# Re-ordering the front of a two-layer attention and expert kernel: clears, gate, row units and part loads

## The reference

```python
xn = _layernorm(x, axis=-1)
# attention, 16 heads of 16, causal
qkv = einsum('bsh,oh->bso', xn, w_qkv)            # q, k, v
scores = einsum('bhqd,bhkd->bhqk', q, k) * scale  # causal mask, softmax, times v, times w_o
# experts: 16 of them, 2 for each token
gate_scores = sigmoid(xn @ Wg.T + balance_bias)
topk_scores, topk_idx = lax.top_k(gate_scores, 2)
topk_scores = topk_scores / (topk_scores.sum(-1, keepdims=True) + 1e-06)
h = silu(einsum('td,edh->teh', xn, W1))
out = einsum('teh,te,ehd->td', h, combine, W2)
x = x + attention + experts
```

## Time and profile before

| | us |
|---|---|
| median of three runs | 1037.07 (1036.24 to 1037.13) |
| the profiled execution, its own time | 1040.66 |
| its span, first to last instruction | 1038.9 |
| PE busy | 903.0 (87% of the span) |
| DVE busy | 659.5 (63%) |
| ACT busy | 424.8 (41%) |
| POOL busy | 360.2 (35%) |
| mean granted TensorE clock | 0.93 of full |

### The profile page before, as it was taken

The page is one execution under the profiler, slowest core; times in us unless marked ns, Lnnn a source line. Parts: engine busy times, 40 slices in busy tenths (PEclk is TensorE's granted clock), DMA queues, the critical chain, the costliest instruction groups (busy, mean ns, idle before and its releaser), DMA issues. The chain is left out here.

```text
span 1038.9 us, 18184 instructions
## 1 busy us (share of the span) xinstructions
PE 903.0 (87%) x5962; PEld 482.8 (46%) x5963; DVE 659.5 (63%) x1561; ACT 424.8 (41%) x736; POOL 360.2 (35%) x541
## 2 busy tenths in 40 slices
PE   5577889999999999999999988889982799997763
PEld 3342223344444444444443322667440687786552
DVE  4257899887777787887877942758132444444444
ACT  3251245565655556555556666221120233331000
POOL 2121127413443325424242373002776000002775
PEclk9797589999999999999999989979997899999787
DMA  4855746230137312191110121900222354453443
GB/s 129 287 140 154 197 67 198 74 118 32 58 78 168 128 32 62 41 199 54 34 41 22 51 73 59 342 2 23 104 101 96 116 159 153 151 153 101 131 128 115
DMA packets 84136, 113.50 MB, mean 109 GB/s; under 512 B 12694, under 2 KB 72086, under 8 KB 83542
## 3 DMA queue, kind: packets, MB, share of 16 engines
q1 hardware_dynamic: 60966, 63.77, 21.8%
q0 software_dynamic: 13728, 37.50, 11.4%
q10 hardware_dynamic: 9360, 11.17, 3.3%
HBM read 58.11 MB, written 54.00 MB: 108 GB/s over the span
## 5 line engine op out<-in xcount | busy, mean ns | idle before, releaser
L732 ACT ACTIVATE probs<-ps_st 128x1024 f32<-128x1024 f32 (+3 forms) x320 | 286.2, 896 | 229.9 <-PE ps_st L1006 227.9
L856 DVE TENSOR_REDUCE part_max<-ps_row 128x1 f32<-128x512 f32 (+3 forms) x560 | 349.8, 668 | 46.7 <-PE ps_row L1022 23.4
L918 PE MATMUL ps_o<-probs,v_all 128*17 128x256 f32 (+1 forms) x2432 | 178.9, 367 | 2.8 <-POOL probs L629 2.5
L1226 POOL DMA_INDIRECT moe_yg<-yd,slot x64 | 61.5, 961 | 168.6 <-DMA yd<-moe_ys 149.4
L1022 PE MATMUL ps_row<-ks,qs 96*128 96x512 bf16 (+3 forms) x320 | 99.9, 377 | 16.7 <-DVE part_max L856 15.6
L1376 POOL DMA_INDIRECT xd<-xn,slot x64 | 64.0, 1000 | 91.6 <-DVE slot L209 72.5
L629 POOL TENSOR_SCALAR_AFFINE_SELECT probs<-probs 128x256 f32<-128x256 f32 x128 | 52.3, 411 | 125.2 <-ACT probs L732 124.0
L1022 PE MATMUL ps_row<-xt_ks,qs 96*128 96x512 bf16 (+3 forms) x320 | 92.5, 348 | 2.3 <-DVE part_max L856 0.9
L1006 PE MATMUL ps_st<-qs,ks 99*128 99x512 bf16 (+3 forms) x320 | 89.3, 362 | 4.4 <-DMA qs<-max_parts 4.4
L1006 PE MATMUL ps_st<-qs,xt_ks 99*128 99x512 bf16 (+3 forms) x320 | 88.1, 358 | 0.0
L918 PEld LDWEIGHTS ps_o<-probs,v_all 128*17 128x17 f32 x2432 | 40.7, 95 | 97.5 <-issue 88.4
(11 more groups left out here) (220 smaller groups left out, 1308.6 us busy)
## 6 DMA issues: line engine op xcount, KB each, us to landing
moe_xs<-xd SPq DMA_DIRECT2D x79, 128.0 KB, 2.1
yd<-moe_ys SPq DMA_DIRECT2D x79, 128.0 KB, 2.0
xd<-zeros SPq DMA_DIRECT2D x4, 2048.0 KB, 8.5
qk_parts<-probs SPq DMA_DIRECT2D x16, 384.0 KB, 4.1
qs<-qk_parts SPq DMA_DIRECT2D x96, 64.0 KB, 2.5
moe_xs<-xd POOLq DMA_DIRECT2D x47, 128.0 KB, 2.4
yd<-moe_ys POOLq DMA_DIRECT2D x47, 128.0 KB, 2.1
xd<-zeros ACTq DMA_DIRECT2D x2, 2048.0 KB, 13.0
```

The source lines that it names most:

```text
L732: act.activation(probs[:, at % NPB, :, off:CH], ps_st[at % 2][:, :, off:CH], ACT.Exp, scale=HD ** -0.5).then_inc(exp_done, 1)
L856: dve.tensor_reduce(part_max[reduced % 2][:, h:h + k, i, j:j + 1], bank[:, 0:k * w].rearrange("p (h w) -> p h w", h=k), AX_X, ALU.max).the ...
L918: mm = pe.matmul(ps_o[32 * q:32 * q + HD + 1, lo:hi], m.v_all[:, k, g * HG + q, :], probs[:, (at + q // 2) % NPB, q % 2, lo:hi], start=Fal ...
L1226: pool.indirect_dma_start(out=yg[:, i % YG, k, :], out_offset=None, in_=yd, in_offset=bass.IndirectOffsetOnAxis(m.r["slot"][:, k, i:i + 1], 0)
```

## The change

- **Clears.** The zeroing of `xd0` moves from ACT, after block 3, to SP, right behind the loads of x. The expert weights w1 and w2 are loaded by ACT at the start, behind the other weights, no longer after block 15.
- **Gate by chunk.** Bias, exponential, reciprocal, MAX8 and FIND_INDEX8 run for 4 tiles at a time. ACT makes the exponentials of chunks 0 and 1 ahead of the turned tokens of chunk 3, that of chunk 2 ahead of chunk 3's values, that of chunk 3 behind block 8.
- **Row units alternate with blocks.** Block 8 stands before row 0, 9 before row 3, 10 before row 6, 11 before row 9, 12 before row 11, 13 before row 13, 14 and 15 before row 16.
- **`rows_out(0, 0)`** is issued by ACT, between blocks 13 and 14, no longer by SP.
- **Parts by chunk.** `qk_parts` is laid out by part, chunk, output, token, and the outputs of a group are ordered position before head (the weights are reordered on the host), so a partition's load is one run of 4 KB. Terms that are neighbours are loaded together: three DMAs (of 3, 2 and 1 terms) for the keys of a chunk of the first group and three for the queries of a chunk of any group. Keys of later groups still take six DMAs.

```diff
+K_RUNS = [(0, 3), (3, 2), (5, 1)]
+Q_RUNS = [(0, 3, 0), (3, 2, 1), (5, 1, 2)]
+LOADS = len(K_RUNS)
...
-def load_keys(eng, m, g, tokens, done):
+def load_keys(eng, m, g, done):
+    rows = slice(D + g * HG * HD, D + (g + 1) * HG * HD)
     for t in range(TERMS):
-        src = m.qk_parts[K_PART[t], D + g * HG * HD:D + (g + 1) * HG * HD, tokens]
-        eng.dma_start(m.ks[g % 2][t * HD:(t + 1) * HD, :, tokens], src.rearrange("(h d) t -> d h t", d=HD)).then_inc(done, 16)
+        eng.dma_start(m.ks[g % 2][t * HD:(t + 1) * HD, :, :, :].rearrange("d c h t -> d c (h t)"),
+                      m.qk_parts[K_PART[t], :, rows, :].rearrange("c (d h) t -> d c (h t)", h=HG)).then_inc(done, 16)
+def load_chunk_of_keys(eng, m, g, c, done):
+    rows = slice(D + g * HG * HD, D + (g + 1) * HG * HD)
+    for first, count in K_RUNS:
+        eng.dma_start(m.ks[g % 2][first * HD:(first + count) * HD, c, :, :].rearrange("d h t -> d (h t)"),
+                      m.qk_parts[0:count, c, rows, :].rearrange("r (d h) t -> r d (h t)", h=HG)).then_inc(done, 16)
 def load_queries(eng, m, g, c, done):
-    for t in range(TERMS):
-        src = m.qk_parts[Q_PART[t], g * HG * HD:(g + 1) * HG * HD, c * CH:(c + 1) * CH]
-        eng.dma_start(m.qs[c][t * HD:(t + 1) * HD, :, :], src.rearrange("(h d) t -> d h t", d=HD)).then_inc(done, 16)
+    rows = slice(g * HG * HD, (g + 1) * HG * HD)
+    for first, count, part in Q_RUNS:
+        src = m.qk_parts[part, c, rows, :].rearrange("(d h) t -> d (h t)", h=HG)
+        eng.dma_start(m.qs[c][first * HD:(first + count) * HD, :, :].rearrange("d h t -> d (h t)"),
+                      src.unsqueeze(0).to_broadcast([count, HD, HG * CH])).then_inc(done, 16)
 def load_first_group(eng, m, c):
     for n in range(4 * c, 4 * c + 4):
         eng.wait_ge(m.parts_out[n], 16)
-    load_keys(eng, m, 0, slice(c * CH, (c + 1) * CH), m.first_in[c])
+    load_chunk_of_keys(eng, m, 0, c, m.first_in[c])
     load_queries(eng, m, 0, c, m.first_in[c])
 CLEAR = 16
-HEAD = 11
 TURNED = 16
+BLOCKS_BEFORE_ROW = {0: [8], 3: [9], 6: [10], 9: [11], 11: [12], 13: [13], 16: [14, 15]}
...
-    m.qk_parts = m.scratch("qk_parts", [PARTS, 2 * D, S], BF16)
+    m.qk_parts = m.scratch("qk_parts", [PARTS, C, 2 * D, CH], BF16)
...
+            sp.wait_ge(zero_ready, 1)
+            clear(sp, m, m.xd0, 0, NT0, m.cleared[0])
...
-                if n == 4 * C - 3:
-                    rows_out(0, 0)
...
+            act.dma_start(m.w1[:, :, :, :], a["w1"].rearrange("(k p) (e h) -> p k e h", p=P, e=E)).then_inc(m.moe0_w_in, 16)
+            act.dma_start(m.w2[:, :, :], a["w2"].rearrange("e p d -> p e d")).then_inc(m.moe0_w_in, 16)
...
-            act.wait_ge(zero_ready, 1)
-            clear(act, m, m.xd0, 0, NT0, m.cleared[0])
             turned_tokens(1)
             root(3)
             values_and_gate(1)
@@ -710,14 +731,18 @@
                 high_and_mid(n)
             turned_tokens(2)
             values_and_gate(2)
+            exp_of_gate(0)
+            exp_of_gate(1)
             turned_tokens(3)
+            exp_of_gate(2)
             values_and_gate(3)
-            act.wait_ge(logit_ready, 1)
-            act.activation(scores[:, :, :], scores[:, :, :], ACT.Exp, scale=-1.0).then_inc(exp_ready, 1)
-            for n in range(8, 16):
+            high_and_mid(8)
+            exp_of_gate(3)
+            for n in range(9, 14):
                 high_and_mid(n)
-            act.dma_start(m.w1[:, :, :, :], a["w1"].rearrange("(k p) (e h) -> p k e h", p=P, e=E)).then_inc(m.moe0_w_in, 16)
-            act.dma_start(m.w2[:, :, :], a["w2"].rearrange("e p d -> p e d")).then_inc(m.moe0_w_in, 16)
+            rows_out(act, 0, 0)
+            high_and_mid(14)
+            high_and_mid(15)
...
+            def gate_best(c):
+                cs = slice(c * TC, (c + 1) * TC)
+                dve.wait_ge(exp_ready, c + 1)
+                step.then(dve.tensor_scalar(scores[:, cs, :], scores[:, cs, :], 1.0, None, ALU.add))
+                step.then(dve.reciprocal(scores[:, cs, :], scores[:, cs, :]))
+                route_best(dve, step, r, scores, range(c * TC, (c + 1) * TC))
+            def before_row(n):
+                for block in BLOCKS_BEFORE_ROW.get(n, []):
+                    rest_of(block)
+                    if block == 8:
+                        gate_logits(C - 1)
+                    if block == 9:
+                        gate_best(C - 1)
+                    if block in (10, 11, 12):
+                        next(routing)
+                    if block == 13:
+                        route_to("masks")
+                    if block == 15:
+                        route_to("weights")
...
-                    pe.wait_ge(m.first_in[c], 16 * 2 * TERMS)
+                    pe.wait_ge(m.first_in[c], 16 * 2 * LOADS)
                     return
-                pe.wait_ge(q_in[c], 16 * TERMS * g)
+                pe.wait_ge(q_in[c], 16 * LOADS * g)
...
+                for block in BLOCKS_BEFORE_ROW.get(n, []):
+                    project_block(block)
```

More of the change, by code:

```diff
@@ L123, in norm_apply, with route_best @@
     step.sync()
+def route_best(dve, step, r, scores, tiles):
+    for i in tiles:
+        step(dve.max(r["best"][:, i, :], scores[:, i, :]))
+    step.sync()
+    for i in tiles:
+        step(dve.max_index(r["arg"][:, i, :], r["best"][:, i, :], scores[:, i, :]))
+    step.sync()
 def route(dve, step, r, scores, top, tiles, eps, factor, masks_ready, ranks_ready, ranks, slots_ready, ranks_read=None):
     best, arg, argf = r["best"], r["arg"], r["argf"]
[L132 to L139, removed]
     step.then(dve.tensor_copy(argf[:, :, :], arg[:, :, :]))
@@ L505, in used, with rows_out @@
             return sum(u[0] != "h" for u in rows[:n + 1])
+        def rows_out(eng, n, c):
+            eng.wait_ge(parts_ready, n + 1)
+            for part in range(PARTS):
+                eng.dma_start(qs[c][KROWS + part:KROWS + part + 1, :, :].rearrange("r h t -> r (h t)"),
+                              max_parts[n % 2][:, part, :]).then_inc(rows_in[n % 2], 16)
         @block.sync
         def _(sp):
[L510 to L514, removed]
             for c in range(C):
@@ L687, in values_and_gate, with exp_of_gate @@
                     act.copy(scores[:, i, :], ps_v[i % 2][:, D:D + E]).then_inc(v_copied, 1)
+            def exp_of_gate(c):
+                cs = slice(c * TC, (c + 1) * TC)
+                act.wait_ge(logit_ready, c + 1)
+                act.activation(scores[:, cs, :], scores[:, cs, :], ACT.Exp, scale=-1.0).then_inc(exp_ready, 1)
             def high_and_mid(n):
@@ L788, in before_plan @@
                 dve.wait_ge(b_in, 16)
-                dve.wait_ge(v_copied, T)
-                dve.tensor_tensor(scores[:, :, :], scores[:, :, :], bias.unsqueeze(1).to_broadcast([P, T, E]),
-                                  ALU.add).then_inc(logit_ready, 1)
[L792 to L808, removed]
-                if n == TURNED:
-                    rest_of(14)
-                    rest_of(15)
-                    route_to("weights")
+                for c in range(C - 1):
+                    gate_logits(c)
@@ new lines, in before_plan, with gate_logits @@
+                for c in range(C - 1):
+                    gate_best(c)
+            def gate_logits(c):
+                cs = slice(c * TC, (c + 1) * TC)
+                dve.wait_ge(v_copied, (c + 1) * TC)
+                dve.tensor_tensor(scores[:, cs, :], scores[:, cs, :], bias.unsqueeze(1).to_broadcast([P, TC, E]),
+                                  ALU.add).then_inc(logit_ready, 1)
+            def gate_best(c):
+                cs = slice(c * TC, (c + 1) * TC)
+                dve.wait_ge(exp_ready, c + 1)
+                step.then(dve.tensor_scalar(scores[:, cs, :], scores[:, cs, :], 1.0, None, ALU.add))
+                step.then(dve.reciprocal(scores[:, cs, :], scores[:, cs, :]))
+                route_best(dve, step, r, scores, range(c * TC, (c + 1) * TC))
@@ L829, in _ @@
                 n += 1
-                between_blocks(n)
+                before_row(n)
                 if u[0] == "h":
@@ L978, in _ @@
                 project_values(c)
-            for n in range(8, 12):
-                project_block(n)
             for u in plan:
-                if state["row"] == HEAD and state["exp"] == 0:
-                    project_block(12)
-                    project_block(13)
-                if state["row"] == TURNED and state["exp"] == 0:
-                    project_block(14)
-                    project_block(15)
                 if u[0] == "exp":
@@ L1477, in _ @@
                                         peak[:, :].unsqueeze(2).to_broadcast([P, T, E]), ALU.mult))
+            route_best(dve, step, r, scores, range(T))
             for _ in route(dve, step, r, scores, TOP1, NT1, 0.0, TOP1 / (TOP1 + 1), masks_ready, ranks_ready, 1,
@@ L1689, in experts_last, with width_before_head @@
         return w.transpose(1, 0, 2).reshape(w.shape[1], -1)
+    def width_before_head(w_t):
```

(4 more changed lines are left out.)

20 lines of the change are left out of this document (10 added, 10 removed).

## The result

| | before | after |
|---|---|---|
| median, us | 1036.65 (1035.38 to 1037.13) | 1053.66 (1049.5 to 1055.73) |
| ratio, 95% interval | | 1.0161 [1.0128, 1.0194] |
| profiled execution, its own time | 1040.66 | 1049.5 |
| its span | 1038.9 | 1047.8 |

The change costs 17 us. The forecast of 1037.5 and its range of 1027 to 1042 both miss it. The profiled execution of after is 4.2 us under its median, that of before 4.0 over it: the two traces differ by 8.9 us where the medians differ by 17.0. The other 8.1 us belong to these two executions and not to the change, and no row says where in the front or behind the attention they lie. Inside the attention, from exp unit 60 on, the difference between two traces stays constant to 0.1 us over dozens of units.

What follows compares the result with a forecast made beforehand. The front bounds what can change: ACT held by clears, DVE, PE and ACT waiting in turns, a 4.40 us wait at the first exp. Terms +0.6, +3.6, -3.5 and -0.3 sum to +0.4: 1037.5 us, range 1027 to 1042.

Steps and rivals of the forecast that it cites:

- Clears on SP: Front: the stall moves to block 0's parts; high part 4 at 44.5 (41 to 47), chunk 2's first copy at 54.2, -0.8 us.
- Gate by chunk and rows between blocks: Front: gate +1.7 and -0.3 us; block 8's remainder to the turn 29.0 for 25.4, +3.6, with 7.5 idle at row 11.
- Row maxima on ACT: Turn to first exp: 11.4 in place of 14.95 us, -3.5; the 4.40 wait goes, block 14's hold-up costs +1.1.
- The first exp: End of the front: first exp at 108.7 where it was 108.01, the sum +0.6 + 3.6 - 3.5 = +0.7 us.
- Behind it: After the first exp: same work in the same order, later loads hidden, slightly less traffic at the first exps; -0.3 us.
- Twice nothing waits soon.: Later query loads, 5.5 us in place of 1.1 on one engine: at two places nothing behind them is wanted soon.
- 8.5 us; after, 1 + 5.5 + 1 is 7.5 ... I take 0.: Maxima behind queries at a group's first chunk: 7.5 us needed, 8.5 available; three times 0 to 1 us, taken as 0.
- Rival C: Steady stage: narrow loads or POOL's expert loads delay the maxima, three groups lose 1 to 2 us each; +6, 1043; chance 0.15.

Runs made afterwards that it cites:

- wide loads: The changed kernel, but keys of a chunk and queries each loaded by six one-term DMAs of outer dimension 16: 1026.97 us, ratio 0.9905.
- clears alone: The kernel before, with only the clears moved to SP and w1 and w2 loaded at the start: 1028.68 us, ratio 0.9916.
- clears as before: The changed kernel with six-DMA loads of outer dimension 16, clears on ACT behind block 3 and expert weights behind block 15: 1029.44 us, ratio 0.9941.
- maxima behind blocks 14 and 15: The changed kernel with six-DMA loads of outer dimension 16, ACT issuing the row maxima after blocks 14 and 15's high and mid parts: 1022.23 us, ratio 0.987.
- the run with two clears on SP: The best kernel, with two clears on SP behind the loads of x and the third on ACT behind chunk 3's turned tokens: 1104.17 us, ratio 0.9849.
- the best kernel: The changed kernel with six-DMA loads of outer dimension 16 and row maxima issued behind blocks 14 and 15: 1022.23 us, ratio 0.987.

## Why the prediction was wrong

**Clears on SP.** Right in kind: the stall moved to the landing of the parts. The size was 3.4 us too pessimistic, 41.09 for 44.5. The term that failed is the rate: I put 13.26 MB at the 346 to 349 GB/s of the earlier trace rows, and the mixed queues ran at 386 (20 to 36 us), which takes 3.8 us off the sum. The prediction had 41 as its bound for this. Chunk 2's first copy came at 49.76 for 54.2.

**Gate by chunk and rows between blocks.** From the remainder of block 8 to the turn it is 27.7 us (63.88 to 91.55) for 29.0. The wait at row 11 was 8.31 for 7.5, and the half clock behind it came too (3.21 us for block 13). Row 11 itself came 19.8 us behind the remainder for 20.0. That this is so near is in part luck: of the 11.0 us that I gave the narrow loads, 5.5 for each half, the runs show 3.8 and 2.5 against wide loads, which are themselves 2.09 us late where I had nothing late. For the same reason the 19.7 us to the turn with wide loads agree only by chance with my 19.8 for data that are never late.

**Row maxima on ACT.** Turn to first exp on PE is 11.7 for 11.4. The sum was right and its causes half wrong: the 4.40 us of the earlier trace rows are gone as soon as the expert weights are out of the way, with the maxima still on SP (clears alone), and also when ACT issues the maxima ahead of those weights (clears as before). And the hold-up of block 14, priced at 1.1, cost 3.3 (maxima behind blocks 14 and 15).

**The first exp** came at 103.26 for 108.7, so the front was better than forecast by 5.4 us, most of it the 3.4 of high part 4.

**Behind it**: here the prediction failed, with +18.4 for -0.3. Two steps:

- "Twice nothing waits soon." The two query loads issued together late in a group are indeed wanted late. But in SP's list the keys of the next group stand behind them, and I never priced those: 4.6 and 4.2 us. The earlier trace rows is the one place of SP's list that I had looked at.
- "8.5 us; after, 1 + 5.5 + 1 is 7.5 ... I take 0." From the issue of the queries at 257.00 to PE's row at 266.89 it took 9.9 us. In the trace the first packet of SP's queue moves at 258.5 and the last of the maxima at 265.6, so the three terms are 1.5, 7.1 and 1.3. A 4 KB packet of these loads took 0.16 us when least disturbed, 26 GB/s, so the rate was not too high; but between 258.5 and 263 many took 0.2 to 0.75. What slowed them is likely POOL's expert traffic in the same stretch, which C had named; no run shows it. The three places lost 3.0, 4.2 and 2.3, not 0 to 1 each: the waits were 1.67, 2.68 and 2.23, and behind the first two the clock took more, a term that I had not put there at all.

Rival C had this mechanism and the place of the maxima, at 1 to 2 us each and a chance of 0.15. They measured 9.5 in all, and the keys, which it did not have, 8.8. The margin of 1 us on which I took 0 rested on a start-up, a rate and a landing that no row of before showed for a narrow load; with these unknown, the waits behind it should have been priced at both ends and summed over all five places.

The packets of after show that the reading of the earlier trace rows was right. Queue rows of 256.9 to 266.5 us:

```profile
q1 hardware_dynamic: 213, 0.41, 15.9%
```

One chunk's queries are 96 packets, one for each partition. Three maxima DMAs of 16 partitions are 32 each, 16 of them extra, so 96. That leaves 21: 3, 2 and 16, one for each engine used. The load of a single term, whose outer dimension of 1 falls away, ran on all 16. The Trainium skill (DMA: Bandwidth & Descriptors, "Why a DMA increments its semaphore by 16 and not by 1") has the engine count follow the slowest dimensions that are not 1; the trace agrees, with 3, 2 and 16 extra packets. The 27 GiB/s for an engine that the prediction quotes from the Trainium skill's Specifications is 29 GB/s, more than the 26 of the fastest packets here.

## What to carry to other kernels

Count engines, not DMAs: three loads with outer dimensions 3, 2 and 1 replaced six with 16, moved the same bytes, and cost 26.7 us (1026.97 to 1053.66). When a load gets slower, go down the issuing engine's list from every place where it stands and price each DMA behind it; re-ordering two of them took back 17 of those us with the slow loads untouched. A wait of 2 to 3 us on PE cost up to 4.6, since the clock was low behind it. And gains do not add up: 7.7 and 6.8 us alone made 9.4 together, most likely because both edits remove the same wait.

## What the runs showed of the hardware that I had not expected

- Two queues together, one writing zeros and one loading weights, ran at 386 GB/s (after, 20 to 36 us), where the clears alone had 346 to 349.
- An earlier start is not kept where PE's clock falls: 16 value matmuls took 5.52 us where it read 0.50 (1.2 of 2.4 GHz) and 3.83 at full clock, though PE had idled 2.2 us before them in both kernels. What decided between the two is open.
- While the keys of a group (1.5 MB, outer dimension 16) are loaded, all engines are busy at less than half the rate of the clears, in before (152 and 149 GB/s from 310 to 318 us) as in after (100 and 128 in the same stretches). No run shows why. Before, in 310 to 314 us, columns as above:

```profile
310.00:314.00 4.00, 3.45 (x33) 1.68 (x33) 2.81 (x6) 1.77 (x4) 0.98 (x2) 1.00 1.02 152
```

- In one set of runs the whole kernel took 8% longer, though the first exp of nearly the same kernel came within 0.7 us (91.17 and 90.92 against 91.54). Part of the excess is in single long waits: the run with two clears on SP has one of 6.64 us on PE at 166.82 that the trace puts down to "issue", where the best kernel has none over 1.7 between 100 and 200 us. The cause is open.
